# Two small products between gather and output as three products of split operands, on one core

## The chip, the cores and the metric

The kernel runs on one core of a Trainium2 chip. The metric is the device time of one execution in microseconds (us). The engines are TensorE (PE; its weight loads are PEld), VectorE (DVE), ScalarE (ACT), GpSimd (POOL) and SyncE (SP), which issues all DMAs here. Each engine works through its own instructions in the order in which they are written and waits on semaphores for the others.

## The reference, cut to what matters

```python
def _gn(v, G=32, eps=1e-5):                      # group norm over (h, w, 8 channels of a group)
    g = v.reshape(B_, H_, W_, G, C_ // G)
    m = jnp.mean(g, axis=(1, 2, 4), keepdims=True)
    s = jnp.var(g, axis=(1, 2, 4), keepdims=True)
    return ((g - m) / jnp.sqrt(s + eps)).reshape(v.shape)

def conv(x, W_qkv, W_out, b_out):                # x: (16, 64, 64, 256), n = 4096 positions
    qkv = jnp.einsum('bhwc,cd->bhwd', x, W_qkv)
    q, k, v = jnp.split(qkv, 3, axis=-1)         # each to (b, 256, n)
    k = jax.nn.softmax(k, axis=-1)               # over the n positions
    context = jnp.einsum('bdn,ben->bde', k, v)
    out = jnp.einsum('bde,bdn->ben', context, q)
    return jnp.einsum('bhwc,cd->bhwd', out, W_out) + b_out

y = x + conv(_gn(x), W_qkv, W_out, b_out)
```

## The kernel before, in words

The 16 images are done one after the other, as a software pipeline. An image has 4096 positions in 8 chunks of 512 (four tiles of 128), and 256 channels in two halves of 128.

For each image the kernel forms the keys from the raw x with the norm's scale put into the key weights (`wk_hi`, `wk_lo`), takes the exponential of keys less a running maximum (`e_hi`, `e_lo`), and sums exp(keys) times x over positions (the gather). The result, 256 x 256, times `Wq` (`combine_u`) and times `Wv Wout` (`combine_m`, whose weights `wvo` are multiplied out once at the start), plus the identity, is one matrix m. The output is x times m plus a bias. Wherever precision is needed, a factor is split into a high part rounded to fp32r and the rest, and a product is three fp32r products: high by high, low by high, high by low. This holds for the keys (L325 to L360), the gather (L390 to L413) and the output (L447 to L470). The two combines (L419 to L436) are plain fp32 products: `acc` (fp32) by `wq_r`, and `u_sb` (fp32) by `wvo_r`.

TensorE's order in one period (L494 to L533): gather of image b, 8 chunks, with the turning of the second block's maximum in it; keys of chunk 0 of the next image n; `combine_u`; two tiles of keys of chunk 1; `combine_m`; the other two tiles; then output chunks of b and key chunks of n in turn. In the last period there are no keys.

ScalarE splits x and its transpose (`x_hi`, `xt_hi`), copies keys out of PSUM (`keys_out`), does the exponentials, scales `wk`, `wvo` and `wq` (L567 to L584), and adds the output's bias. GpSimd subtracts to get `xt_lo` and `x_lo`; in each period it waits at L315 for `wk_ready` (VectorE's `wk_low`) before the third `xt_low` of the next image, and its order is written out (L305 to L320). VectorE takes the running maximum of keys in `mx`, 512 wide (L731 to L739, two operations a chunk, each waiting for the one before), restarted every four chunks (a block). At the end of a block TensorE turns `mx` with four transposes (L362 to L370), VectorE reduces them to one maximum per channel (L745), and TensorE spreads it (L372). VectorE also shifts the keys (L759), forms `e_lo`, the statistics of the image after next (L693), and the small matrices: `take_second` (L781) leaves `rz` and `acc`, `take_u` (L800) `u_sb`, `take_m` (L808) `m_hi`, `m_full` and `m_lo`.

SP loads the statistics' slots `xs` as VectorE frees them (`bn_done`).

Of the kernel before, what the change touches and what calls it, by code (L numbers as in the profile page):

```python
# [11 lines left out]
P = 128  # L12
# [16 lines left out]
def build(nc: bass.Bass, xt: bass.AP, xn: bass.AP, w: bass.AP, b_out: bass.AP, out: bass.AP):  # L29
# [11 lines left out]
    with ExitStack() as ctx:  # L41
# [33 lines left out]
        wq_t = sb("wq_t", [P, CB, C])  # L75
        wq_r = sb("wq_r", [P, CB, C])
        wvo = sb("wvo", [P, CB, C])
        wvo_r = sb("wvo_r", [P, CB, C])
# [9 lines left out]
        mx = sb("mx", [P, 2 * C])  # L88
        acc = sb("acc", [P, CB, C])
        m_full = acc  # L90
        m_hi = sb("m_hi", [P, CB, C], F32R)
# [3 lines left out]
        m_lo = sb("m_lo", [P, CB, C], F32R)  # L95
# [44 lines left out]
        wvo_r_ready = sem("wvo_r_ready")  # L140
# [22 lines left out]
        wq_r_ready = sem("wq_r_ready")  # L163
# [97 lines left out]
        def _(pool):  # L261
# [64 lines left out]
        def _(pe):  # L326
# [6 lines left out]
            def keys_high(b, parity, j, t0, t1):  # L333
                if t0 == 0:
                    pe.wait_ge(xt_hi_ready, b * NCH + (j + 1))
                    if j == 0:
                        pe.wait_ge(wk_ready, b + 1)
                    if j >= 2:
                        pe.wait_ge(max_done, b * (2 * NCH) + (2 * j - 2))
# [22 lines left out]
            def turn_max(b, blk):  # L362

                to = (ps_g0, ps_k[:, 0])[blk]
                pe.wait_ge(max_done, b * (2 * NCH) + (NCH * blk + NCH))
# [53 lines left out]
            def combine_u(b):  # L419
                pe.wait_ge(wq_r_ready, b * CB + CB)  # L420
                for c in range(CB):
                    for d in range(CB):
                        if c == 0:
                            pe.wait_ge(acc_ready, b * CB + (d + 1))
                        last = nc.tensor.matmul(ps_g0[:, c, 0:C], acc[:, d, c * P:(c + 1) * P], wq_r[:, d, :],  # L425
                                                start=(d == 0), stop=(d == CB - 1))
                    last.then_inc(u_ps, 1)

            def combine_m(b):
                pe.wait_ge(wvo_r_ready, b + 1)  # L430
                pe.wait_ge(u_ready, b + 1)
                for i in range(CB):
                    for c in range(CB):
                        last = nc.tensor.matmul(ps_g0[:, i, 0:C], u_sb[:, c, i * P:(i + 1) * P], wvo_r[:, c, :],  # L434
                                                start=(c == 0), stop=(c == CB - 1))
                    last.then_inc(m_ps, 1)  # L436
# [49 lines left out]
            for j in range(2, NCH):  # L486
                keys(0, 0, j)
                if j == 4:
                    pe.wait_ge(setup_sb, 2)
                    turn_max(0, 0)  # L490
                elif j == 5:
                    spread_max(0, 0)
# [46 lines left out]
        def _(act):  # L539
# [27 lines left out]
            def wvo_scaled(b, parity):  # L567
                act.wait_ge(rstd_ready, b + 1)
                for c in range(CB):
                    last = nc.scalar.activation(wvo_r[:, c, :], wvo[:, c, :], ACT.Copy,  # L570
                                                scale=rstd[:, parity, c:c + 1])
                last.then_inc(wvo_r_ready, 1)

# [6 lines left out]
            def wq_scaled(b):  # L580
                act.wait_ge(rz_ready, b + 1)
                for d in range(CB):
                    nc.scalar.activation(wq_r[:, d, :], wq_t[:, d, :], ACT.Copy,
                                         scale=rz[:, d:d + 1]).then_inc(wq_r_ready, 1)  # L584
# [17 lines left out]
            for j in range(X_SLOTS):  # L602
# [3 lines left out]
                if j == 1:  # L606
                    act.wait_ge(setup_ps, 1)
                    nc.scalar.activation(wvo[:], ps_g0[:, :, 0:C], ACT.Copy).then_inc(setup_sb, 1)
                    act.wait_ge(setup_ps, 2)
                    nc.scalar.activation(wq_sum[:], ps_e[:, 0, 0:C], ACT.Copy).then_inc(setup_sb, 1)  # L610
            act.wait_ge(setup_sb, 2)
# [6 lines left out]
            def period(b, parity, more, more2):  # L618
# [16 lines left out]
                wvo_scaled(b, parity)  # L635
# [6 lines left out]
                wq_scaled(b)  # L642
                if more:
                    keys_out(n, 0, 0)
                    x_high(n, 0)
                    keys_out(n, 0, 1)
                    x_high(n, 1)
# [39 lines left out]
        def _(dve):  # L687
# [43 lines left out]
            def key_max(b, j, h):  # L731
                dve.wait_ge(k_out, b * (2 * NCH) + (2 * j + h + 1))
                if j % HALF == 0 and h == 0:
                    if j or not (isinstance(b, int) and b == 0):
                        dve.wait_ge(t_ps, b * 2 + j // HALF)
                    nc.vector.tensor_copy(mx[:], ps_k[:, j % 2, h, :]).then_inc(max_done, 1)
                    return
                dve.wait_ge(max_done, b * (2 * NCH) + (2 * j + h))
                nc.vector.tensor_tensor(mx[:], ps_k[:, j % 2, h, :], mx[:], ALU.max).then_inc(max_done, 1)  # L739
# [55 lines left out]

            def mean_bias(b, parity):
# [3 lines left out]
            def take_u(b, parity):  # L800
                for c in range(CB):
                    dve.wait_ge(u_ps, b * CB + (c + 1))
                    last = nc.vector.scalar_tensor_tensor(out=u_sb[:, c, :], in0=wq_sum[:],  # L803
                                                          scalar=neg_mean[:, parity, c:c + 1], in1=ps_g0[:, c, 0:C],
                                                          op0=ALU.mult, op1=ALU.add)
                last.then_inc(u_ready, 1)
# [30 lines left out]
            for j in range(HALF):  # L837
                key_maxes(0, j)
                for q in range(2 * j, 2 * j + 2):
                    bn_half(1, q)  # L840
            for q in range(8, 12):
                bn_half(1, q)
# [18 lines left out]
            def period(b, parity, more, more2):  # L861
# [88 lines left out]
```

## Time and profile before

| | us |
|---|---|
| median of 3 runs | 1262.89 (1261.8 to 1263.22) |
| the profiled execution's own time | 1263.93 |
| its span, first to last instruction | 1262.2 |
| granted TensorE clock, mean | 0.996 of full |
| VectorE busy | 879.4 (70%) |
| ScalarE busy | 839.1 (66%) |
| GpSimd busy | 657.4 (52%) |
| DMA | 266.69 MB, mean 211 GB/s |

Times in the trace are from the span's start. In the rows of a timeline, a line is a run of alike instructions: its start, the time from its start to its last end, the engine, the source line, what is written and read, the shapes, and the count. A bracket at the end is the time for which the engine was idle before it, and what released it. Matmuls are pipelined, so a record's duration is longer than its distance to the next.

### The profile page before, as it was taken

The numbers are of one execution on the slowest core, as the hardware profiler recorded it, in microseconds if no ns is written. First come the engines' busy times: TensorE is split into PE (matmuls) and PEld (weight loads), VectorE is DVE, ScalarE is ACT, GpSimd is POOL, SyncE is SP. The second block draws the span as 40 slices with busy tenths as digits, with TensorE's granted clock in tenths as the row PEclk, the third lists the DMA queues.
The fourth block names the chain that finished last, engine by engine and source line by source line (L and its number), as shares of the span: only waits on it lengthen the run. The fifth ranks groups of instructions, "written<-read, shape, count | busy, mean of one in ns | idle before, by whom it ended". The sixth has DMA issues, their size and how long they took to land. (4 is left out here: it accounts for less than half of the span.)

```text
span 1262.2 us, 21236 instructions
## 1 busy us (share of the span) xinstructions
PE 1220.6 (97%) x8396; PEld 1132.2 (90%) x8396; DVE 879.4 (70%) x1264; ACT 839.1 (66%) x1139; POOL 657.4 (52%) x284
## 2 busy tenths in 40 slices
PE   3899999999999999999999999999999999999998
PEld 3798999989999898999989999899999989999886
DVE  5877767877677776767777577676776777577461
ACT  4476857767576776857767576775756768576663
POOL 7274653836546374553736547364563736537320
PEclk9899999999999999999999999999999999999999
DMA  8247657486665867657486564866657576573523
GB/s 332 85 167 267 215 192 245 151 300 217 215 220 170 281 200 258 204 185 260 163 294 209 206 227 157 293 217 236 203 180 265 185 271 219 190 241 118 190 92 134
DMA packets 109107, 266.69 MB, mean 211 GB/s; under 512 B 12240, under 2 KB 12240, under 8 KB 109008
## 3 DMA queue, kind: packets, MB, share of 16 engines
q1 hardware_dynamic: 109008, 265.34, 62.1%
q8 instruction: 66, 1.08, 0.3%
q14 instruction: 33, 0.27, 0.1%
HBM read 198.18 MB, written 67.11 MB: 210 GB/s over the span
## 5 line engine op out<-in xcount | busy, mean ns | idle before, releaser
L283 POOL TENSOR_TENSOR xt_lo<-xt_raw,xt_hi 128x1024 fp32r<-128x1024 f32 x128 | 307.0, 2401 | 496.1 <-ACT xt_hi L543 462.3
L289 POOL TENSOR_TENSOR x_lo<-x_raw,x_hi 128x1024 fp32r<-128x1024 f32 x128 | 324.3, 2548 | 67.5 <-ACT x_hi L548 67.4
L594 ACT ACTIVATE o_stage<-ps_e,bias 128x512 f32<-128x512 f32 x256 | 172.8, 689 | 125.6 <-PE ps_e L463 125.6
L770 DVE TENSOR_TENSOR e_lo<-e_raw,e_hi 128x1024 fp32r<-128x1024 f32 x128 | 251.6, 1966 | 3.1 <-ACT e_raw L561 2.2
L739 DVE TENSOR_TENSOR mx<-ps_k,mx 128x512 f32<-128x512 f32 x224 | 154.7, 691 | 120.6 <-ACT e_raw L552 108.5
L552 ACT ACTIVATE e_raw<-ps_k 128x512 f32<-128x512 f32 x256 | 142.1, 596 | 131.6 <-PE ps_k L328 131.6
L328 PE MATMUL ps_k<-wk_hi,xt_hi 128*128 128x256 f32 x1024 | 214.5, 291 | 3.8 <-DVE wk_lo L725 3.0
L328 PE MATMUL ps_k<-wk_lo,xt_hi 128*128 128x256 f32 x1024 | 207.2, 284 | 0.0
L560 ACT ACTIVATE e_hi<-e_raw 128x1024 fp32r<-128x1024 f32 x128 | 135.0, 1055 | 66.7 <-PE ps_g L409 36.8
L698 DVE BATCH_NORM_STATS2 bn<-xs 128x6 f32<-128x512 f32 x240 | 153.4, 686 | 35.3 <-DMA xs<-in_xt_dram 34.9
L328 PEld LDWEIGHTS ps_k<-wk_hi,xt_hi 128*128 128x128 f32 x1024 | 166.7, 191 | 12.5 <-issue 4.0
L455 PE MATMUL ps_e<-xt_hi,m_hi 128*128 128x512 f32 x512 | 162.3, 398 | 0.6 <-DVE m_hi L811 0.6
L463 PE MATMUL ps_e<-xt_hi,m_lo 128*128 128x512 f32 x512 | 162.1, 398 | 0.0
L455 PE MATMUL ps_e<-xt_lo,m_hi 128*128 128x512 f32 x512 | 160.9, 395 | 0.0
L328 PEld LDWEIGHTS ps_k<-wk_lo,xt_hi 128*128 128x128 f32 x1024 | 159.2, 190 | 0.0
L328 PE MATMUL ps_k<-wk_hi,xt_lo 128*128 128x256 f32 x1024 | 158.5, 283 | 0.0
L548 ACT ACTIVATE x_hi<-x_raw 128x1024 fp32r<-128x1024 f32 x128 | 134.5, 1051 | 17.5 <-DMA x_raw<-in_xn_dram 17.4
L543 ACT ACTIVATE xt_hi<-xt_raw 128x1024 fp32r<-128x1024 f32 x128 | 134.9, 1054 | 4.7 <-DMA xt_raw<-in_xt_dram 4.7
L328 PEld LDWEIGHTS ps_k<-wk_hi,xt_lo 128*128 128x128 f32 x1024 | 137.9, 190 | 0.0
L400 PE MATMUL ps_e<-x_hi,e_hi 128*128 128x258 f32 x512 | 128.8, 290 | 8.7 <-POOL x_lo L289 7.0
L561 ACT ACTIVATE e_raw<-e_raw 128x1024 f32<-128x1024 f32 x128 | 134.1, 1048 | 0.0
L400 PE MATMUL ps_g<-x_hi,e_hi 128*128 128x258 f32 x512 | 126.7, 284 | 3.6 <-issue 3.6
(81 smaller groups left out, 1875.2 us busy)
## 6 DMA issues: line engine op xcount, KB each, us to landing
xt_raw<-in_xt_dram SPq DMA_DIRECT2D x128, 512.0 KB, 4.6
x_raw<-in_xn_dram SPq DMA_DIRECT2D x128, 512.0 KB, 3.4
out_dram<-o_stage SPq DMA_DIRECT2D x256, 256.0 KB, 4.6
xs<-in_xt_dram SPq DMA_DIRECT2D x240, 256.0 KB, 5.0
w_setup<-in_w_dram SPq DMA_DIRECT2D x2, 256.0 KB, 9.7
wk<-in_w_dram SPq DMA_DIRECT2D x1, 256.0 KB, 9.8
wq_t<-in_w_dram SPq DMA_DIRECT2D x1, 256.0 KB, 9.8
b_col<-in_b_out_dram SPq DMA_DIRECT2D x1, 1.0 KB, 9.9
```

The source lines that it names most:

```text
L283: nc.gpsimd.tensor_tensor(xt_lo[:, s], xt_raw[:, s], xt_hi[:, s].bitcast(F32), ALU.subtract).then_inc(xt_lo_ready, 1)
L289: nc.gpsimd.tensor_tensor(x_lo[:, s], x_raw[:, s], x_hi[:, s, :, 0:C].bitcast(F32), ALU.subtract).then_inc(x_lo_ready, 1)
L328: return nc.tensor.matmul(ps_k[:, j % 2, t // 2, (t % 2) * C:(t % 2 + 1) * C], (xt_hi, xt_lo)[xs_][:, slot(j, parity), c, t * P:(t + 1) * ...
L400: nc.tensor.matmul(ps_g[j // HALF][:, d, 0:C + 2], w_, x_hi[:, j % X_SLOTS, t, :], start=(j % HALF == 0 and t == 0), stop=False, skip_grou ...
L455: nc.tensor.matmul(ps_e[:, h, :], m_hi[:, c, h * P:(h + 1) * P], x_[:, s, c, :], start=(n == 0 and c == 0), stop=False, skip_group_check=True)
L463: last = nc.tensor.matmul(ps_e[:, h, :], m_lo[:, c, h * P:(h + 1) * P], xt_hi[:, s, c, :], start=False, stop=(c == CB - 1), skip_group_che ...
L552: nc.scalar.activation(e_raw[:, j, 2 * h:2 * h + 2, :].rearrange("p t c -> p (t c)"), ps_k[:, j % 2, h, :], ACT.Copy).then_inc(k_out, 1)
L560: nc.scalar.activation(e_hi[:, j % E_SLOTS], e_raw[:, j], ACT.Exp).then_inc(e_hi_ready, 1)
L594: nc.scalar.activation(o_stage[:, q % O_SLOTS, :], ps_e[:, h, :], ACT.Identity, bias=bias[:, h:h + 1]).then_inc(o_ready, 1)
L698: nc.vector.bn_stats(bn[:, q % CB, q // CB, :], xs[:, q % S_SLOTS, :]).then_inc(bn_done, 1)
L739: nc.vector.tensor_tensor(mx[:], ps_k[:, j % 2, h, :], mx[:], ALU.max).then_inc(max_done, 1)
L770: nc.vector.tensor_tensor(e_lo[:, j], e_raw[:, j], e_hi[:, j % E_SLOTS].bitcast(F32), ALU.subtract).then_inc(e_lo_ready, 1)
```

## The change

`combine_u` and `combine_m` become three fp32r products each: the left side is split into `acc_hi` and `acc_lo` (`u_hi` and `u_lo`), the right side is split once at the start (`wq_hi`, `wq_lo`, `wvo_hi`, `wvo_lo`). The scales 1/z and rstd, which were put on the right sides in each image by ScalarE, are put on the left sides as they are split: ScalarE writes the high part, VectorE then the low part. GpSimd's wait before the third `xt_low` is for `u_lo_ready` in place of `wk_ready`. The running maximum is 256 wide: four operations a chunk for two, and two transposes a block for four. At the start ScalarE also writes `wq_hi`, and VectorE does two subtractions for `wvo_lo` and `wq_lo`.

```diff
@@ gpsimd, period
-                    pool.wait_ge(wk_ready, n + 1)
+                    pool.wait_ge(u_lo_ready, b * CB + CB)
                     xt_low(n, np_, 2)
@@ tensor
             def turn_max(b, blk):
                 for d in range(CB):
-                    for h in range(2):
-                        last = nc.tensor.transpose(to[:, 0, (2 * d + h) * P:(2 * d + h + 1) * P],
-                                                   mx[:, h * C + d * P:h * C + (d + 1) * P], ident)
+                    last = nc.tensor.transpose(to[:, 0, d * P:(d + 1) * P], mx[:, d * P:(d + 1) * P], ident)
             def combine_u(b):
-                pe.wait_ge(wq_r_ready, b * CB + CB)
                 for c in range(CB):
                     for d in range(CB):
                         if c == 0:
-                            pe.wait_ge(acc_ready, b * CB + (d + 1))
-                        last = nc.tensor.matmul(ps_g0[:, c, 0:C], acc[:, d, c * P:(c + 1) * P], wq_r[:, d, :],
-                                                start=(d == 0), stop=(d == CB - 1))
+                            pe.wait_ge(acc_hi_ready, b * CB + (d + 1))
+                        for w_ in (wq_hi, wq_lo):
+                            nc.tensor.matmul(ps_g0[:, c, 0:C], acc_hi[:, d, c * P:(c + 1) * P], w_[:, d, :],
+                                             start=(d == 0 and w_ is wq_hi), stop=False, skip_group_check=True)
+                for c in range(CB):
+                    for d in range(CB):
+                        if c == 0:
+                            pe.wait_ge(acc_lo_ready, b * CB + (d + 1))
+                        last = nc.tensor.matmul(ps_g0[:, c, 0:C], acc_lo[:, d, c * P:(c + 1) * P], wq_hi[:, d, :],
+                                                start=False, stop=(d == CB - 1), skip_group_check=True)
                     last.then_inc(u_ps, 1)
             (combine_m likewise, with u_hi, u_lo, wvo_hi, wvo_lo)
@@ scalar
-            def wvo_scaled(b, parity): ...
-            def wq_scaled(b): ...
+            def acc_high(b):
+                act.wait_ge(rz_ready, b + 1)
+                for d in range(CB):
+                    act.wait_ge(acc_ready, b * CB + (d + 1))
+                    nc.scalar.activation(acc_hi[:, d, :], acc[:, d, :], ACT.Copy,
+                                         scale=rz[:, d:d + 1]).then_inc(acc_hi_ready, 1)
+            def u_high(b, parity):
+                for c in range(CB):
+                    act.wait_ge(u_ready, b * CB + (c + 1))
+                    nc.scalar.activation(u_hi[:, c, :], u_sb[:, c, :], ACT.Copy,
+                                         scale=rstd[:, parity, c:c + 1]).then_inc(u_hi_ready, 1)
@@ scalar, period
-                wvo_scaled(b, parity)
-                wq_scaled(b)
+                acc_high(b)
                 if more:
                     keys_out(n, 0, 0)
                     x_high(n, 0)
                     keys_out(n, 0, 1)
+                u_high(b, parity)
@@ vector
             def key_max(b, j, h):
                 dve.wait_ge(k_out, b * (2 * NCH) + (2 * j + h + 1))
+                for t in (2 * h, 2 * h + 1):
+                    tile = ps_k[:, j % 2, h, (t % 2) * C:(t % 2 + 1) * C]
+                    if j % HALF == 0 and t == 0:
+                        if j or b:
+                            dve.wait_ge(t_ps, b * 2 + j // HALF)
+                        nc.vector.tensor_copy(mx[:], tile).then_inc(max_done, 1)
+                    else:
+                        dve.wait_ge(max_done, b * (TILES * NCH) + (TILES * j + t))
+                        nc.vector.tensor_tensor(mx[:], tile, mx[:], ALU.max).then_inc(max_done, 1)
+            def acc_low(b):
+                for d in range(CB):
+                    dve.wait_ge(acc_hi_ready, b * CB + (d + 1))
+                    nc.vector.scalar_tensor_tensor(out=acc_lo[:, d, :], in0=acc[:, d, :], scalar=rz[:, d:d + 1],
+                                                   in1=acc_hi[:, d, :].bitcast(F32), op0=ALU.mult,
+                                                   op1=ALU.subtract).then_inc(acc_lo_ready, 1)
+            (u_low likewise, from u_sb, rstd and u_hi)
@@ vector, period
                 take_second(b)
+                acc_low(b)
                 if more:
                     key_max(n, 0, 0)
                 take_u(b, parity)
                 if more:
                     key_max(n, 0, 1)
+                u_low(b, parity)
                 take_m(b, parity)
@@ vector, start, after chunk 1
+                    nc.vector.tensor_tensor(wvo_lo[:], ps_g0[:, :, 0:C], wvo_hi[:].bitcast(F32), ALU.subtract)
+                    nc.vector.tensor_tensor(wq_lo[:], wq_t[:], wq_hi[:].bitcast(F32), ALU.subtract)
```

## Rows read from the trace of the kernel before

**Rows 1.** The page's first part: busy us, share, instructions of each engine.
```profile
PE 1220.6 (97%) x8396; PEld 1132.2 (90%) x8396; DVE 879.4 (70%) x1264; ACT 839.1 (66%) x1139; POOL 657.4 (52%) x284
```
**Rows 2.** TensorE's waits (total, times, longest), and busy times of one image's stretch.
```profile
PE ps_e L400 <- POOL x_lo L289: 7.0, 15, 0.7
...
594.03:670.20 76.17, 75.62 (x525) 70.24 (x524) 55.06 (x80) 52.11 (x71) 41.24 (x17) 1.00 0.66 221
```
**Rows 3.** Timeline of TensorE around the two combines of one image.
```profile
619.64 0.40 PE L328 MATMUL ps_k<-wk_hi,xt_hi 128*128 128x256 f32 x2
...
622.48 1.89 PE L425 MATMUL ps_g<-wq_r,acc 128*128 128x256 f32 x8
624.02 0.59 PE L328 MATMUL ps_k<-wk_hi,xt_hi 128*128 128x256 f32 x2
624.44 0.40 PE L328 MATMUL ps_k<-wk_lo,xt_hi 128*128 128x256 f32 x2
...
629.72 0.95 PE L442 MATMUL ps_g<-neg_mean,acc 128*128 128x1 f32 x8
630.52 0.71 PE L463 MATMUL ps_e<-xt_hi,m_lo 128*128 128x512 f32 x2
```
**Rows 4.** Timeline of TensorE at both turns of the maximum.
```profile
595.95 0.60 PE L368 MATMUL ps_k<-zero_eye,mx 128*128 128x128 f32 x4
596.38 0.28 PE L384 MATMUL ps_k<-mv,grp 128*128 128x2 f32 x2
...
646.63 0.60 PE L368 MATMUL ps_g<-zero_eye,mx 128*128 128x128 f32 x4
```
**Rows 5.** Timeline of VectorE in one image, and in the last.
```profile
609.40 1.90 DVE L770 TENSOR_TENSOR e_lo<-e_raw,e_hi 128x1024 fp32r<-128x1024 f32 x1
...
617.53 0.87 DVE L725 SCALAR_TENSOR_TENSOR wk_lo<-wk,rstd,wk_hi 128x256 fp32r<-128x256 f32 x2
...
620.30 0.85 DVE L793 SCALAR_TENSOR_TENSOR acc<-ps_e,alpha,acc 128x256 f32<-128x256 f32 x2
...
624.41 0.48 DVE L803 SCALAR_TENSOR_TENSOR u_sb<-wq_sum,neg_mean,ps_g 128x256 f32<-128x256 f32 x1 [0.39 <-PE ps_g L425]
...
628.93 1.26 DVE L822 TENSOR_TENSOR m_lo<-acc,m_hi 128x512 fp32r<-128x512 f32 x1
...
644.18 1.49 DVE L739 TENSOR_TENSOR mx<-ps_k,mx 128x512 f32<-128x512 f32 x2 [2.38 <-ACT e_raw L552]
...
667.83 1.49 DVE L739 TENSOR_TENSOR mx<-ps_k,mx 128x512 f32<-128x512 f32 x2 [2.76 <-ACT e_raw L552]
...
1236.22 0.69 DVE L822 TENSOR_TENSOR m_lo<-acc,m_hi 128x512 fp32r<-128x512 f32 x1
```
**Rows 6.** Timeline of ScalarE after a gather.
```profile
620.42 0.91 ACT L583 ACTIVATE wq_r<-wq_t,rz 128x256 f32<-128x256 f32 x2 [4.26 <-DVE rz L790]
621.26 0.60 ACT L552 ACTIVATE e_raw<-ps_k 128x512 f32<-128x512 f32 x1
```
**Rows 7.** Groups by form: count, busy us, mean ns of one, idle before.
```profile
L739 DVE TENSOR_TENSOR mx<-ps_k,mx 128x512 f32<-128x512 f32 x224 | 154.7, 691 | 120.6 <-ACT e_raw L552 108.5 <-DVE mx L739 0.5
...
L776 DVE TENSOR_TENSOR z<-ps_g,alpha 128x2 f32<-128x2 f32 x16 | 2.4, 147 | 1.2 <-PE ps_g L409 1.2
```
**Rows 8.** Timeline of GpSimd in the same image.
```profile
608.01 8.51 POOL L289 TENSOR_TENSOR x_lo<-x_raw,x_hi 128x1024 fp32r<-128x1024 f32 x3
618.48 2.40 POOL L283 TENSOR_TENSOR xt_lo<-xt_raw,xt_hi 128x1024 fp32r<-128x1024 f32 x1 [1.96 <-DVE wk_lo L725]
...
627.45 2.19 POOL L289 TENSOR_TENSOR x_lo<-x_raw,x_hi 128x1024 fp32r<-128x1024 f32 x1 [0.23 <-ACT x_hi L548]
...
640.06 2.41 POOL L283 TENSOR_TENSOR xt_lo<-xt_raw,xt_hi 128x1024 fp32r<-128x1024 f32 x1 [7.24 <-ACT xt_hi L543]
```
**Rows 9.** Timeline of image 0: VectorE's fourth shift, TensorE's first gather.
```profile
56.55 1.22 DVE L764 TENSOR_TENSOR e_raw<-e_raw,ps_g 128x1024 f32<-128x1024 f32 x1
...
57.87 0.55 PE L400 MATMUL ps_g<-x_hi,e_hi 128*128 128x258 f32 x1 [3.58 <-issue]
```

More of the change, by code:

```diff
@@ L74, in build @@
         wk_lo = sb("wk_lo", [P, CB, C], F32R)
[L75 to L78, printed above, removed]
+        with nc.sbuf_tensor("wq_t", [P, CB, C], F32) as wq_t:
+            pass
+        wq_lo = sb("wq_lo", [P, CB, C], F32R)
+        wq_hi = sb("wq_hi", [P, CB, C], F32R)
+        wvo_hi = sb("wvo_hi", [P, CB, C], F32R)
+        wvo_lo = sb("wvo_lo", [P, CB, C], F32R)
         wq_sum = sb("wq_sum", [P, C])
@@ L86, in build @@
         grp = sb("grp", [P, P])
-        mx = sb("mx", [P, 2 * C])
-        acc = sb("acc", [P, CB, C])
+        mx = sb("mx", [P, C])
+        with nc.sbuf_tensor("acc", [P, CB, C], F32) as acc:
+            pass
+        acc_lo = sb("acc_lo", [P, CB, C], F32R)
         m_full = acc
-        m_hi = sb("m_hi", [P, CB, C], F32R)
+        acc_hi = sb("acc_hi", [P, CB, C], F32R)
+        m_hi = acc_hi
         with nc.sbuf_tensor("u_sb", [P, CB, C], F32) as u_sb:
             pass
-        m_lo = sb("m_lo", [P, CB, C], F32R)
+        u_lo = sb("u_lo", [P, CB, C], F32R)
+        u_hi = sb("u_hi", [P, CB, C], F32R)
+        m_lo = u_lo
         bn = sb("bn", [P, CB, NCH, 6])
@@ L162, in build @@
         rz_ready = sem("rz_ready")
-        wq_r_ready = sem("wq_r_ready")
+        acc_hi_ready = sem("acc_hi_ready")
+        acc_lo_ready = sem("acc_lo_ready")
+        u_hi_ready = sem("u_hi_ready")
+        u_lo_ready = sem("u_lo_ready")
+        setup_lo = sem("setup_lo")
         acc_ready = sem("acc_ready")
@@ L431, in combine_m @@
-                pe.wait_ge(u_ready, b + 1)
                 for i in range(CB):
                     for c in range(CB):
-                        last = nc.tensor.matmul(ps_g0[:, i, 0:C], u_sb[:, c, i * P:(i + 1) * P], wvo_r[:, c, :],
-                                                start=(c == 0), stop=(c == CB - 1))
+                        if i == 0:
+                            pe.wait_ge(u_hi_ready, b * CB + (c + 1))
+                        for w_ in (wvo_hi, wvo_lo):
+                            nc.tensor.matmul(ps_g0[:, i, 0:C], u_hi[:, c, i * P:(i + 1) * P], w_[:, c, :],
+                                             start=(c == 0 and w_ is wvo_hi), stop=False, skip_group_check=True)
@@ L436, in combine_m @@
+                for i in range(CB):
+                    for c in range(CB):
+                        if i == 0:
+                            pe.wait_ge(u_lo_ready, b * CB + (c + 1))
+                        last = nc.tensor.matmul(ps_g0[:, i, 0:C], u_lo[:, c, i * P:(i + 1) * P], wvo_hi[:, c, :],
+                                                start=False, stop=(c == CB - 1), skip_group_check=True)
                     last.then_inc(m_ps, 1)
@@ L489, in _ @@
                     pe.wait_ge(setup_sb, 2)
+                    pe.wait_ge(setup_lo, 1)
                     turn_max(0, 0)
@@ L565, in scales @@
                 nc.scalar.activation(alpha[:], dm[:], ACT.Exp).then_inc(alpha_ready, 1)
[L567 to L572, printed above, removed]
             def wk_high(b, parity):
@@ L646, in period @@
                     keys_out(n, 0, 1)
+                u_high(b, parity)
+                if more:
                     x_high(n, 1)
@@ L802, in take_u, with u_low @@
                     dve.wait_ge(u_ps, b * CB + (c + 1))
[L803 to L806, printed above, removed]
+                    nc.vector.scalar_tensor_tensor(out=u_sb[:, c, :], in0=wq_sum[:],
+                                                   scalar=neg_mean[:, parity, c:c + 1], in1=ps_g0[:, c, 0:C],
+                                                   op0=ALU.mult, op1=ALU.add).then_inc(u_ready, 1)
+            def u_low(b, parity):
+                for c in range(CB):
+                    dve.wait_ge(u_hi_ready, b * CB + (c + 1))
+                    nc.vector.scalar_tensor_tensor(out=u_lo[:, c, :], in0=u_sb[:, c, :],
+                                                   scalar=rstd[:, parity, c:c + 1],
+                                                   in1=u_hi[:, c, :].bitcast(F32), op0=ALU.mult,
+                                                   op1=ALU.subtract).then_inc(u_lo_ready, 1)
             def take_m(b, parity):
```

32 lines of the change are left out of this document (15 added, 17 removed).

## The prediction

> **What bounds the kernel now.** I read the busy shares first, then TensorE's waits, then one middle image engine by engine. TensorE is busy 97% of the span [rows 1], and its waits are few: the only one that recurs is 7.0 us in 15 waits for `x_lo`, 0.45 us an image [rows 2]. From one gather's start to the next an image takes 76.17 us, 75.62 of them TensorE work at the full clock [rows 2]. So two questions decide: how much TensorE time the edits take out of an image, and whether the longer chains through ScalarE and VectorE still arrive before TensorE asks for them.
>
> **TensorE work removed.** Key matmuls (fp32r, 256 wide) go at 24 in 622.48 - 619.64 = 2.84 us, 0.118 us each [rows 3]. `combine_u`, four fp32 products, starts at 622.48; the third matmul after it starts at 624.44. Less the two before that (0.24), it costs 1.72 us [rows 3]. Twelve fp32r products of the same width cost 12 x 0.118 = 1.42. Saving 0.30 us each, 0.60 an image. `turn_max` takes 0.43 us for four transposes, up to the next matmul [rows 4]; two less save 0.21, two times an image 0.43. Bounds: the combines save 0.12 if the records' own distance counts (1.54 - 1.42, 624.02 less 622.48), 0.30 with the change-over into fp32r that follows; the transposes 0.18 to 0.21. I take the upper ends, since TensorE's next work starts by them. Together 1.03 us an image.
>
> The Trainium skill, "FP8 and Floating Point Precision", TensorE Precision Notes, says that true FP32 takes four passes through the array. By that four products are 16 passes against 12, and the ratio 16/12 on 1.42 would make the old combine 1.89 and the saving 0.47; the row says 1.72, and the sum goes by the row.
>
> **The chain into `combine_u`.** `rz` comes just before `acc`, which runs 620.30 to 621.15 in two halves [rows 5], and ScalarE's scaled copies take 0.91 for two [rows 6]. New order: `acc_hi` 620.8-621.3 and 621.2-621.7, `acc_lo` on VectorE (two of this kind and width take 0.87 [rows 5]) 621.3-622.2. TensorE asks for `acc_hi` at 622.48 and for `acc_lo` 0.95 later, so 0.6 us and more is to spare: no cost. The cover is the four tiles of keys; without it about 1.9 us would show. ScalarE's `keys_out(n,0,0)` slips from 621.26 [rows 6] to 621.6, and `wvo_scaled` disappears, where ScalarE then idled anyway: nothing on the path.
>
> **The chain into `combine_m`.** The product's second half comes out at 622.48 + 1.42 + 0.2 (as the gather's end reaches VectorE, 619.84 against 619.64) = 624.10. `take_u` is 0.48 a half [rows 5]: 623.9-624.35 and 624.27-624.75. `u_hi` on ScalarE 624.4-624.9, 624.8-625.3; TensorE asks at 625.32 (623.90 + two tiles of keys): in time. Behind `take_u` VectorE still has `key_max(n,0,1)`. No row has a 128x256 maximum; by the 128x512 one (0.691) and the 128x2 operation (0.147) [rows 7] it is 0.42 to 0.43, plus 0.11 from one to the next, which waits for it (two of 0.69 span 1.49 [rows 5]). Two of them: 624.67-625.64. Then `u_lo` 625.56-626.43. TensorE has done its eight high products and one low one at 625.32 + 9 x 0.118 = 626.39 and needs the second half of `u_lo` then, which reaches it at 626.48 to 626.57: a wait of 0.1 to 0.2, with a slow restart of 0.07. I take 0.2 us in each of 15 images. Bounds: 0 if the narrow maximum takes half of 0.691 (0.35), 0.7 if it takes all of it.
>
> **GpSimd, moved behind `u_lo`.** It started `xt_low(n,2)` at 618.48 [rows 8], now at 626.5. Everything on its queue behind that moves too: four `x_low` of 2.2 and `xt_low(n,3)`. 2.4 + 0.6 + 4 x 2.2 puts it free at 638.3; `xt_low(n,3)` waited 7.24 us for ScalarE until 640.06 [rows 8]. SP issues nothing in this step that waits for GpSimd. No cost from lateness, but the order matters for `m_lo`. Two-input SBUF operations of VectorE and GpSimd's subtractions never share a stretch here: `e_lo` took 1.90 when it started at 609.40 [rows 5], within GpSimd's three `x_lo` of 8.51 us from 608.01 [rows 8]: 0.8 of waiting for the one in flight, then 1.1 of work, while the next one stood. `m_lo` likewise took 1.26 at 628.93 against 0.69 in the last image, where GpSimd is idle [rows 5]; the `x_lo` in flight ended at 629.64 [rows 8].
>
> Now call T the end of `u_lo`. GpSimd's `xt_lo` runs T+0.08 to T+2.47. TensorE resumes at T+0.1, `m_hi`'s halves end at T+0.98 and T+1.38, the two `m_full` at T+2.17, `m_lo` is issued at T+2.27: 0.2 us before GpSimd's instruction ends. It goes next and is done at T+3.0. TensorE asks for it at T+0.53 (combine over) + 1.42 (keys) + 0.94 + 0.80 (high products and bias sum, 628.78 to 630.52 in this image, [rows 3] has the bias sum's start and the end) = T+3.7. No cost, and 0.6 us earlier than today.
>
> The Trainium skill, "SBUF — State Buffer", Who interferes with whom, states this as a rule: a VectorE instruction with two SBUF inputs contends with a GpSimd one that reads SBUF, and issue order decides who blocks. The durations above agree. By it `acc_lo` and `u_lo` are safe, as GpSimd is idle there, and `m_lo` hangs on which GpSimd instruction it meets.
>
> **The narrower maximum on VectorE.** Four operations for two: 3 x 0.54 + 0.43 = 2.05 against 1.49, 0.56 us a chunk, 4.5 an image. VectorE idles 2.76 us before the last chunk's maximum at 667.83 [rows 5]; the chunks whose delay reaches it (4, 5, 6) add 1.7, and the wait shrinks to about 1. Before the first block's turn: chunk 3 starts at 644.18 and would end at 646.23; TensorE turns at 646.63 [rows 4]: 0.3 to spare after 0.14 of signalling. The reduction of a turned block is 0.27 shorter, off the path. No cost in steady state. Upper bound, at 0.69 each: 3.1 a chunk, turn 0.8 late.
>
> **Start.** In image 0 VectorE is the bound: the fourth `shift` at 56.55 lasts 1.22, and TensorE starts the first gather at 57.87 after 3.58 us idle [rows 9]. From the first block's reduction, some 12 us earlier, VectorE is never idle, and three chunks of maxima (+1.7), less 0.3 for the reduction, lie in it. Ahead of it the two set-up subtractions (1.3) and wider maxima delay the statistics that free `xs` slots, by some 0.9. Gather starts 2.3 us later; bounds 1.2 and 4.
>
> **Sum.** 15 full images at -1.03 + 0.2 = -0.83 give -12.5; the last one has no keys for cover, but its added splits overlap its high products: -0.4 with its one `turn_max`. Start +2.3. Together -10.6 us, on the profiled execution's own 1263.93 us (span 1262.2 and 1.7 around it): 1253.3. That execution lies 1.04 above the median of the runs, 1262.89, and the same step from the median gives 1252.3; I say 1253.
>
> **Rivals.**
> (a) `m_lo` misses its turn. If it is issued over 0.2 us later against GpSimd, or GpSimd sooner, it meets `x_low(n,0)`, waits 2.2 us more, ends at T+5.2, and TensorE, at T+3.7, waits 1.65 us with the signalling: 15 x 1.65 = 25, time 1278. For it: the small distance and GpSimd's queue that is now full behind `xt_lo`. Against: both ends hang on the same T, and their durations repeat to 0.02 us. From 0.2 us on it decides. Slower.
> (b) VectorE late. A narrow maximum that costs 0.48 (as the two-scalar operations of this width) and splits that come some tenths later put 0.5 us on the `u_lo` wait and 0.2 on the turn, and 1.5 on the start: 15 x 0.5 + 1.5 = 9 less gain, 1262. For it: `u_lo` is already the last to come. Against: the cheaper two-input rows.
> (c) No wait at all, and the start hidden: 1253.3 - 3 - 1 = 1249. For it, the 0.1 us by which I find the wait; against, that VectorE's order is fixed.
> (d) The change doesn't save: twelve products with their weight loads go at 0.19 like the old records (1.54 for eight): 2.3 against 1.72, +0.6 x 30 = 18, time 1271 with the transposes' saving inside. Against: keys, with a new weight load for each product, hold 0.118.
>
> **Numbers.** Forecast 0.60, (a) 0.13, (b) 0.12, (c) 0.12, (d) 0.03. The forecast's own range is 1250 to 1257; with (c) and (b) 1248 to 1263, leaving out (a) and (d). A difference under 0.2% (2.5 us) can't be told from none. Faster holds forecast, (c) and a third of (b): 0.76; same, most of the rest of (b): 0.07; slower 0.17.
>
> **What would show it.** Distance from `combine_u`'s first product to the next key 1.42 and 12 records in it; a wait of TensorE for `u_lo` of 0.1 to 0.2, some 15 times; the maximum at 0.43; `m_lo` under 1 us and ended before `x_low(n,0)` starts (2 us or more is rival (a)); the first gather at about 60.2; the `x_lo` wait unchanged at 0.45. The prediction is wrong if an image isn't 0.6 to 1.1 us shorter than 76.2.

## The result and the profile after

The changed kernel takes 1252.12 us (median of 4 runs, 1248.38 to 1255.10) against 1262.47 (median of 4, 1261.8 to 1263.22). The ratio is 0.9917, 95% interval 0.9901 to 0.9934. The profiled execution took 1255.10, span 1253.3.

The page's first part answers to [rows 1], the wait and the stretch of one image to [rows 2]. The stretch runs again from one gather's start to the next.

```profile
PE 1210.3 (97%) x8460; PEld 1127.4 (90%) x8460; DVE 932.3 (74%) x1586; ACT 838.0 (67%) x1140; POOL 661.3 (53%) x284
...
PE ps_e L409 <- POOL x_lo L300: 7.2, 15, 0.5
...
587.92:663.12 75.20, 74.62 (x530) 69.61 (x529) 58.48 (x100) 51.98 (x71) 41.58 (x17) 1.00 0.67 224
```

TensorE is still the bound, the `x_lo` wait is still there, and an image is 0.97 us shorter. VectorE has 3.4 us more work in it and none of it shows.

The timeline of TensorE around the turn and the two combines, answering to [rows 3, 4]. In the trace of the changed kernel `acc_hi` also stands for `m_hi` and `u_lo` for `m_lo`, which share their memory.

```profile
589.83 0.38 PE L378 MATMUL ps_k<-zero_eye,mx 128*128 128x128 f32 x2
590.05 0.28 PE L393 MATMUL ps_k<-mv,grp 128*128 128x2 f32 x2
...
616.12 0.28 PE L436 MATMUL ps_g<-wq_hi,acc_hi 128*128 128x256 f32 x1
...
617.08 0.63 PE L442 MATMUL ps_g<-wq_hi,acc_lo 128*128 128x256 f32 x4
617.55 0.39 PE L339 MATMUL ps_k<-wk_hi,xt_hi 128*128 128x256 f32 x2
...
618.97 0.28 PE L452 MATMUL ps_g<-wvo_hi,u_hi 128*128 128x256 f32 x1
...
619.93 0.73 PE L458 MATMUL ps_g<-wvo_hi,u_lo 128*128 128x256 f32 x4
620.50 0.39 PE L339 MATMUL ps_k<-wk_hi,xt_hi 128*128 128x256 f32 x2
```

The turn takes 0.22 us for 0.43. `combine_u` takes 617.55 - 616.12 = 1.43, and the key after it starts at once. `combine_m` takes 1.53: its last four records, 0.73 long in place of 0.63, hold a wait of 0.10 for `u_lo`.

VectorE and GpSimd in the same stretch, answering to [rows 5, 8]:

```profile
618.31 0.88 DVE L767 TENSOR_TENSOR mx<-ps_k,mx 128x256 f32<-128x256 f32 x2
619.10 0.87 DVE L845 SCALAR_TENSOR_TENSOR u_lo<-u_sb,rstd,u_hi 128x256 fp32r<-128x256 f32 x2
...
622.22 0.79 DVE L864 TENSOR_TENSOR u_lo<-acc,acc_hi 128x512 fp32r<-128x512 f32 x1
...
623.91 1.87 DVE L767 TENSOR_TENSOR mx<-ps_k,mx 128x256 f32<-128x256 f32 x4
```
```profile
620.05 2.41 POOL L294 TENSOR_TENSOR xt_lo<-xt_raw,xt_hi 128x1024 fp32r<-128x1024 f32 x1 [9.87 <-DVE u_lo L845]
622.42 9.13 POOL L300 TENSOR_TENSOR x_lo<-x_raw,x_hi 128x1024 fp32r<-128x1024 f32 x4
```

`m_lo` (the `u_lo` of L864) is issued at 622.22, 0.24 us before GpSimd's `xt_lo` ends at 622.46. It waits a tenth of a us and takes 0.79, where it took 1.26 before. The four `x_lo` take 9.13 together, so the first stood behind `m_lo`.

The whole difference of the two profiled executions (1263.93 - 1255.10 = 8.83) splits by the starts of the gathers:

| stretch | before | after | difference |
|---|---|---|---|
| to the first gather | 57.87 | 58.38 | +0.5 |
| 15 images, first gather to last | 1145.59 | 1131.30 | -14.3 |
| last gather to the last matmul's start | 54.86 | 59.78 | +4.9 |

The images gained more than forecast (12.5), and the last image lost what nobody had counted. The first row can't be read from one pair: over the ten traces here whose kernels have the changed start the first gather comes anywhere from 56.64 to 59.63, and the kernel before, with the same start, gave 56.47 in another trace (that of `before with fill` below).

For the last image the granted clock shows why. The first fence is the changed kernel from within its last gather to the end, the second the kernel before at the same distance from its end (TensorE busy, its granted clock, DMA).

```profile
1203.50:1217.00 13.50, 11.30 (x89) 1.00 0.09 33
1217.00:1230.50 13.50, 12.24 (x44) 0.50 0.05 19
1230.50:1249.50 19.00, 19.00 (x83) 0.99 0.47 180
```
```profile
1217.30:1230.80 13.50, 11.33 (x89) 1.00 0.09 34
1230.80:1244.30 13.50, 12.26 (x57) 1.00 0.20 77
```

For 13.5 us TensorE ran at 1.2 in place of 2.4 GHz. It has three waits in the last image alone, where no keys stand between the products:

```profile
PE ps_g L436 <- ACT acc_hi L602: 1.6, 1, 1.6
...
PE ps_g L452 <- ACT u_hi L608: 0.7, 1, 0.7
PE ps_e L479 <- DVE acc_hi L853: 0.6, 1, 0.6
```

Only the first of them lies ahead of the fall. `combine_u` starts at 1216.25, after the 1.62 us wait, and the clock falls within its first products; the two shorter waits come when it is already at half:

```profile
1216.25 0.39 PE L436 MATMUL ps_g<-wq_hi,acc_hi 128*128 128x256 f32 x1 [1.62 <-ACT acc_hi L602]
```
```profile
1216.50:1217.00 0.50, 0.50 (x5) 1.00 0.00 0
1217.00:1217.50 0.50, 0.50 (x5) 0.59 0.00 0
1217.50:1218.00 0.50, 0.50 (x5) 0.50 0.00 0
```

The kernel before waited as long at the same places and kept 2.4 GHz:

```profile
1230.19 1.99 PE L425 MATMUL ps_g<-wq_r,acc 128*128 128x256 f32 x8 [1.58 <-ACT wq_r L583]
1232.85 1.97 PE L434 MATMUL ps_g<-wvo_r,u_sb 128*128 128x256 f32 x8 [0.67 <-DVE u_sb L803]
1235.39 0.73 PE L455 MATMUL ps_e<-xt_hi,m_hi 128*128 128x512 f32 x2 [0.58 <-DVE m_hi L811]
```

### The profile page after: what moved, and what is told of

Same layout as the page of the kernel before. It is cut to its first block, busy times and chain, and to the rows that moved or that the text cites. A ratio compares the mean times of both kernels' runs of the same rounds, so it can differ in the third digit from the quotient of the medians.

```text
span 1253.3 us, 21671 instructions
## 1 busy us (share of the span) xinstructions
PE 1210.3 (97%) x8460; PEld 1127.4 (90%) x8460; DVE 932.3 (74%) x1586; ACT 838.0 (67%) x1140; POOL 661.3 (53%) x284
## 4 chain that ended last, share of the span: by engine, by line
PE 79%; POOL 9%; DMA 4%; ACT 3%; DVE 3%; issue 1%; SPq 0%; ACTq 0%; DVEq 0%; POOLq 0%
PE ps_k L339 28%; PE ps_e L479 19%; PE ps_e L487 10%; POOL x_lo L300 6%; PE ps_e L409 4%; PE ps_e L418 4%; PE ps_e L411 3%; DMA x_raw<-in_xn_dram 3%; POOL rstd L305 2%; POOL xt_lo L294 2%; PE ps_g L418 2%; PE ps_g L409 2%; PE ps_g L411 2%; PE ps_g L452 1%; PE ps_g L436 1%
## 5 line engine op out<-in xcount | busy, mean ns | idle before, releaser
L300 POOL TENSOR_TENSOR x_lo<-x_raw,x_hi 128x1024 fp32r<-128x1024 f32 x128 | 328.2, 2587 | 20.6 <-ACT x_hi L573 20.1
L767 DVE TENSOR_TENSOR mx<-ps_k,mx 128x256 f32<-128x256 f32 x480 | 203.4, 424 | 99.6 <-ACT e_raw L577 78.7
L798 DVE TENSOR_TENSOR e_lo<-e_raw,e_hi 128x1024 fp32r<-128x1024 f32 x128 | 247.4, 1934 | 4.9 <-ACT e_raw L586 4.5
L339 PE MATMUL ps_k<-wk_hi,xt_hi 128*128 128x256 f32 x1024 | 208.6, 285 | 4.2 <-DVE wk_lo L751 3.0
L479 PE MATMUL ps_e<-xt_hi,acc_hi 128*128 128x512 f32 x512 | 163.7, 401 | 1.0 <-DVE acc_hi L853 0.6
L487 PE MATMUL ps_e<-xt_hi,u_lo 128*128 128x512 f32 x512 | 163.1, 400 | 0.0
L479 PE MATMUL ps_e<-xt_lo,acc_hi 128*128 128x512 f32 x512 | 161.6, 397 | 0.0
```

The lines of the kernel that those rows point to most:

```text
L300: nc.gpsimd.tensor_tensor(x_lo[:, s], x_raw[:, s], x_hi[:, s, :, 0:C].bitcast(F32), ALU.subtract).then_inc(x_lo_ready, 1)
L339: return nc.tensor.matmul(ps_k[:, j % 2, t // 2, (t % 2) * C:(t % 2 + 1) * C], (xt_hi, xt_lo)[xs_][:, slot(j, parity), c, t * P:(t + 1) * ...
L479: nc.tensor.matmul(ps_e[:, h, :], m_hi[:, c, h * P:(h + 1) * P], x_[:, s, c, :], start=(n == 0 and c == 0), stop=False, skip_group_check=True)
L487: last = nc.tensor.matmul(ps_e[:, h, :], m_lo[:, c, h * P:(h + 1) * P], xt_hi[:, s, c, :], start=False, stop=(c == CB - 1), skip_group_che ...
L767: nc.vector.tensor_tensor(mx[:], tile, mx[:], ALU.max).then_inc(max_done, 1)
L798: nc.vector.tensor_tensor(e_lo[:, j], e_raw[:, j], e_hi[:, j % E_SLOTS].bitcast(F32), ALU.subtract).then_inc(e_lo_ready, 1)
```

## The experiments

Each run's own median, with the ratio to the kernel before on the same chip. The third number, an image, is the usual distance of two gather starts in the profile; it is 76.18 before and 75.22 after. The last, the end, is the distance from the last gather's start to the last matmul's start, 54.86 before and 59.78 after. Where two values stand for an image, the first is that of the images at full clock and the second that of those with a stretch at half clock. What each run changes is told below the table; a "fill" is matmuls that nobody reads, put into a wait.

| | us | ratio, 95% interval | image | end |
|---|---|---|---|---|
| changed kernel | 1252.12 | 0.9917, 0.9901 to 0.9934 | 75.22 | 59.78 |
| narrow maximum alone | 1257.73 | 0.9962, 0.9950 to 0.9974 | 75.73 | 54.66 |
| split combines alone | 1258.27 | 0.9951, 0.9935 to 0.9968 | 75.57 | 60.13 |
| fill, three waits | 1250.07 | 0.9900, 0.9887 to 0.9913 | 75.23 | 54.81 |
| before with fill | 1262.55 | 0.9999, 0.9990 to 1.0008 | 76.18 | 54.01 |
| fill, first wait | 1249.19 | 0.9888, 0.9874 to 0.9902 | 75.23 | 54.85 |
| maximum after `u_lo` | 1282.79 | 1.0162, 1.0141 to 1.0184 | 76.3 / 77.75 | 59.83 |
| the same, `x_lo` held | 1249.72 | 0.9902, 0.9877 to 0.9927 | 75.11 | 54.80 |
| `m_lo` later | 1297.00 | 1.0272, 1.0253 to 1.0292 | 76.8 / 78.3 | 59.80 |
| GpSimd's wait put back | 1286.35 | 1.0184, 1.0167 to 1.0201 | 76.5 / 78.0 | 59.82 |
| `rstd` later | 1250.97 | 0.9911, 0.9891 to 0.9931 | 75.22 | 54.81 |
| fill, held, `rstd` later | 1249.74 | 0.9894, 0.9879 to 0.9908 | 75.11 | 54.81 |
| fill first, held | 1248.71 | 0.9890, 0.9873 to 0.9906 | 75.11 | 54.82 |

**The two halves.** The kernel before with the new `key_max`, `turn_max` and `block_max` alone:

```diff
-        mx = sb("mx", [P, 2 * C])
+        mx = sb("mx", [P, C])
+                for t in (2 * h, 2 * h + 1): ...          # as in the change
```


> The kernel before with the 256-wide maximum alone. My account: two transposes less at each of 31 turns, 0.21 us each, -6.6; the start +0.5 as in the changed kernel's trace; together -6, and an image of 75.75 us for 76.17. No half-clock stretch in the last image, since the fp32 combines stay. Rival: the narrow maximum is what loses clock or start time (the start +2.3 as I forecast), then -4 or less.

It came to 1257.73, -4.9 against 1262.65. An image is 75.73, -0.45, as two turns of 0.21 say, and the end is unchanged. The first gather came at 58.86, 1.0 later than before where I had said 0.5; that is within what the same start does from run to run (56.64 to 59.63), so it doesn't say why the whole is 4.9 and not 6.

The changed kernel with the wide maximum back, so the split combines alone:

```diff
-        mx = sb("mx", [P, C])
+        mx = sb("mx", [P, 2 * C])
-                        for w_ in (wvo_hi, wvo_lo):
+                        for w_ in (wvo_hi, wq_lo):
```


> The changed kernel with the 512-wide maximum, so the split combines alone (for room the low part of wvo is not kept, combine_m reads the low part of wq in its place: same work, other numbers). My account: 0.30 us at each of 30 combines, -9, and the u_lo wait gone or under 0.1; an image of 75.57. The last image may lose up to 6.7 us at half clock: then -2 to -9 in all. If the half clock belongs to the split combines, it shows here and not with the maximum alone.

An image is 75.57, -0.61: two combines of 0.30. The runs fall into two groups by the mean granted clock: 1252.86 and 1253.07 at 0.997, and four from 1257.73 to 1259.09 at 0.992. The profiled run is one of the four, and in it the half clock lies in the last image (its end is 60.13); that the other three lost it there too is inferred from their mean. So -9.7 where the end keeps its clock, as I had it, and -4.4 in the median, where it doesn't. The half clock comes with the split combines. The two halves add to -1.06 an image, both together give -0.96: the 0.10 left is the `u_lo` wait, which only the two together have.

**The end.** The changed kernel with matmuls that nobody reads in the last image's waits:

```diff
+            def fill(parity, k):
+                for i in range(k):
+                    nc.tensor.matmul(ps_k[:, 1, 0, 0:C], xt_hi[:, slot(4, parity), i % CB, 0:P], wk_hi[:, i % CB, :],
+                                     start=True, stop=True, skip_group_check=True)
                 if more:
                     keys_tiles(n, np_, 0, 0, 4)
+                else:
+                    fill(parity, 12)
                 combine_u(b)
+                (likewise 5 before combine_m, 4 before the output)
```


> The changed kernel, and in the last image alone 12, 5 and 4 extra matmuls whose result nobody reads, put into TensorE's three waits before combine_u, combine_m and the output. If the waits cost the last image its clock (1217 to 1230 at half clock in the changed kernel's trace, 6.7 us), the granted clock stays full there and the time falls to 1246, with a smaller spread over the runs. Rival: the runs' spread (1248 to 1255) is from elsewhere, and the extra work changes nothing or adds up to 1 us.

The end fell back to 54.81 at full clock, -5.0. The median is 1250.07, higher than I expected, since I had taken the whole 6.7 us of half clock off the median, in which only some runs had it, and the end itself had lost 5.0, not 6.7. The intervals of this kernel (0.9887 to 0.9913) and of the changed one (0.9901 to 0.9934) overlap, so the gain is shown by the end's length and by the clocks counted below, not by the medians. The three waits shrank to 0.2, 0.3 and 0.3 us.

> The kernel before with the same extra matmuls in its last image. Its trace held full clock there, so no change within 1 us. If it also becomes faster, its own runs lose clock too and the fill's worth is not a matter of the split combines.

In the kernel before the same fill shows no gain in time: ratio 0.9999 over 11 runs. Its end is 0.85 shorter in the profile than without, which the interval (0.1% either way, 1.2 us) can't exclude.

> The changed kernel with the twelve extra matmuls in the first of the last image's three waits alone. If the first, 1.6 us long, is what costs the clock, the last image holds full clock as with all three filled (1250). If the shorter two matter as much, the half clock comes back in most runs (1255).

Filling the first wait alone is enough, as the place of the fall within the first products says too. This is its stretch over the first products (TensorE busy, granted clock), and the two waits that stay:

```profile
1213.00:1226.50 13.50, 11.68 (x63) 1.00 0.15 58
```
```profile
PE ps_g L452 <- ACT u_hi L619: 0.9, 1, 0.9
...
PE ps_e L479 <- DVE acc_hi L864: 0.7, 1, 0.7
```

Over all kernels with the short combine chain and without fill (changed, split alone, `x_lo` held, `rstd` later), 9 of 20 runs had a mean clock of 0.992 or less, and they are the longest ones of each: 1255.10 and 1253.51 against 1250.72 and 1248.38 in the changed kernel. Of 18 runs with fill none had, and none took over 1252.1. The mean clock is only a sign of it, since every trace also has some half clock before the second image; where the half clock lay is known for the profiled runs, and there it is at the end for the two at 0.992 or less and not for the other two. The kernel before isn't free of it altogether: one of its 46 runs had 0.993 and took 1267.17, 4.2 us over the median of its group, and where its clock fell no trace shows.

**The rival that was priced at 1278.** First the edit that looks like a gain: take the maximum out of `u_lo`'s way.

```diff
                 take_u(b, parity)
+                u_low(b, parity)
                 if more:
                     key_max(n, 0, 1)
-                u_low(b, parity)
```


> The changed kernel with the maximum of the second key tiles moved from before u_lo to after it, on VectorE. u_lo then comes 0.4 us earlier or more, TensorE no longer waits for it. By the exclusive order of VectorE's and GpSimd's two-input subtractions GpSimd starts earlier too, m_lo is issued just after x_low of the next image began, waits 2.2 us for it, and TensorE waits some 1.5 us in each of 15 images: +22, 1274, an m_lo of 2.5 us or more. Rival, if the engines share rather than exclude: -1 to -2 us, 1251.

1282.79, slower by 20.7 us against the kernel before, 31 against the changed one, and 9 more than the 1274 expected. VectorE, GpSimd and TensorE of one image:

```profile
634.00 0.88 DVE L845 SCALAR_TENSOR_TENSOR u_lo<-u_sb,rstd,u_hi 128x256 fp32r<-128x256 f32 x2 [0.19 <-ACT u_hi L608]
...
637.55 2.52 DVE L864 TENSOR_TENSOR u_lo<-acc,acc_hi 128x512 fp32r<-128x512 f32 x1
```
```profile
634.96 2.41 POOL L294 TENSOR_TENSOR xt_lo<-xt_raw,xt_hi 128x1024 fp32r<-128x1024 f32 x1 [9.38 <-DVE u_lo L845]
637.33 4.81 POOL L300 TENSOR_TENSOR x_lo<-x_raw,x_hi 128x1024 fp32r<-128x1024 f32 x2
```
```profile
640.13 0.72 PE L487 MATMUL ps_e<-xt_hi,u_lo 128*128 128x512 f32 x2 [1.01 <-DVE u_lo L864]
...
641.76 1.06 PE L487 MATMUL ps_e<-xt_hi,u_lo 128*128 128x512 f32 x2
642.62 0.63 PE L339 MATMUL ps_k<-wk_hi,xt_hi 128*128 128x256 f32 x2
643.05 0.63 PE L339 MATMUL ps_k<-wk_lo,xt_hi 128*128 128x256 f32 x2
```

`u_lo` ends at 634.88 and releases GpSimd, whose `x_lo` starts at 637.33. `m_lo` is issued at 637.55, 0.2 us too late, and takes 2.52. TensorE waits 1.01. And then, from 641.8, its matmuls stand 0.43 apart by twos in place of 0.24, half clock. That comes in 9 of the last 14 images, which take 77.75; the other 5 take 76.3. So the wait costs 1.1 us an image, by the mechanism expected (I had 1.5), and the clock after it another 1.45 in most, which I hadn't counted.

The same edit, and GpSimd held:

```diff
                     xt_low(n, np_, 2)
+                    pool.wait_ge(m_lo_ready, b + 1)
                     for j in range(X_SLOTS):
```


> The same move, and GpSimd waits for m_lo before x_low of the next image. If the block is m_lo's meeting with x_low, the cost of the last one vanishes and what is left is the u_lo wait saved: -1 to -1.5 us against the changed kernel, m_lo at 0.69 to 0.9. If the move costs for another reason (the maximum being late), the cost stays.

```profile
619.17 0.88 DVE L768 TENSOR_TENSOR mx<-ps_k,mx 128x256 f32<-128x256 f32 x2
...
621.92 0.69 DVE L865 TENSOR_TENSOR u_lo<-acc,acc_hi 128x512 fp32r<-128x512 f32 x1
```
```profile
619.33 2.41 POOL L294 TENSOR_TENSOR xt_lo<-xt_raw,xt_hi 128x1024 fp32r<-128x1024 f32 x1 [9.38 <-DVE u_lo L846]
622.69 4.37 POOL L300 TENSOR_TENSOR x_lo<-x_raw,x_hi 128x1024 fp32r<-128x1024 f32 x2 [0.95 <-DVE u_lo L865]
```

`m_lo` takes 0.69 and an image 75.11, 0.11 less than in the changed kernel. The two kernels differ in one wait, and by 33 us in the medians. Of the 37.1 us between their profiled executions 31.9 lie in the 15 images: one meeting of two instructions, and what the clock makes of it. The other 5.0 are the half clock at the end, which this profile doesn't have. The late maximum itself shows no cost.

From the other side, with `m_lo` pushed back behind other work of VectorE:

```diff
             def take_m(b, parity): ...
                 last.then_inc(m_full_ready, 1)
+                if b < B - 1:
+                    key_max(b + 1, 1, 0)
                 dve.wait_ge(m_hi_ready, b + 1)
```


> The changed kernel with two 256-wide maxima of the next image's chunk 1 moved ahead of m_lo (0.9 us). m_lo, issued 0.24 us before GpSimd's xt_lo ends now, is issued 0.6 us after it and meets x_low(n,0): it ends about 2.2 us later than now, and TensorE waits 1.5 us an image: +22. Rival, without the block: m_lo ends 0.9 later, at the point where TensorE asks for it: +0 to +2.

1297.00, where I had expected 22 more than the changed kernel, 1274. `m_lo` takes 2.34, and TensorE's wait for it is 1.4 us in each of 15 images.

```profile
640.80 2.34 DVE L866 TENSOR_TENSOR u_lo<-acc,acc_hi 128x512 fp32r<-128x512 f32 x1
```
```profile
640.40 6.95 POOL L300 TENSOR_TENSOR x_lo<-x_raw,x_hi 128x1024 fp32r<-128x1024 f32 x3
```

An image at full clock takes 1.54 more than in the changed kernel, 23 us in 15 images, as expected. But 12 of the last 14 images run in part at half clock, at 1.5 us each, and these 18 us I hadn't counted. In this run and in `maximum after u_lo` `m_lo` ends 2.74 us after the start of the `x_lo` that it met, though it was issued 0.40 after that start here and 0.22 there.

And GpSimd's wait as it was before the change:

```diff
-                    pool.wait_ge(u_lo_ready, b * CB + CB)
+                    pool.wait_ge(wk_ready, n + 1)
```


> The changed kernel with GpSimd's wait put back to wk_low (as before the change): xt_low(n,2) early, then x_low(n,0..3) each as x_hi comes. By the intervals of the trace u_lo finds GpSimd idle (619.04 to 619.9) but m_lo, issued at 622.22, meets x_low(n,2) begun at 622.14, and ends at 624.9 where TensorE asks for it at 623.7: +1.3 us an image, +19, 1271. Rival: the moved wait has no effect on time, 1252.

1286.35, for 1271 expected. Again the price of the wait is right, 1.27 us an image at full clock and 19 in 15, and what is missing is the half clock, in 10 of the last 14 images. The groups of waits of these two kernels, in this order:

```profile
PE ps_e L487 <- DVE u_lo L866: 21.1, 15, 1.4
```
```profile
PE ps_e L487 <- DVE u_lo L864: 17.1, 15, 1.2
```

In this last kernel `m_lo` takes 2.67:

```profile
635.44 2.68 DVE L864 TENSOR_TENSOR u_lo<-acc,acc_hi 128x512 fp32r<-128x512 f32 x1
```

Without the moved wait the change would have been slower than before by 1.8%.

**The wait for `x_lo`.** One attempt at the recurring wait of [rows 2]:

```diff
                     x_low(b, j)
-                    if j == HALF and more:
+                    if j == HALF + 1 and more:
                         rstd_of(n, np_)
```


> The changed kernel with GpSimd's rstd of the next image moved from before to after x_low of chunk 5, in the gather. It took 1.67 us there, ahead of the x_lo for which TensorE waits 0.48 us in each of 15 images (and restarts slowly at chunks 6 and 7, 0.2 each). The gather's bound is GpSimd's queue: -0.5 to -0.9 an image, -7 to -13 in all. Rival: the block between e_lo and x_lo moves along and another x_lo becomes late: 0 to -3; or wk_hi comes late on ScalarE: slower.

An image stays at 75.22: the rival came true, another `x_lo` became late. The rows show where the 1.7 us went. GpSimd, free earlier, waits 0.68 for ScalarE's `x_hi` before chunk 5's `x_lo`, and `rstd` then stands ahead of chunk 6's. TensorE's wait of 0.48 at chunk 5 is gone and one of 0.71 at chunk 6 stands in its place; in all it now waits 8.8 us for `x_lo` and 2.1 for ScalarE's `e_hi`, for 7.2 before the edit.

```profile
599.16 2.48 POOL L300 TENSOR_TENSOR x_lo<-x_raw,x_hi 128x1024 fp32r<-128x1024 f32 x1 [0.68 <-ACT x_hi L573]
601.59 1.69 POOL L305 TENSOR_TENSOR rstd<-var_eps,neg_half 128x2 f32<-128x2 f32 x1
```
```profile
PE ps_e L409 <- POOL x_lo L300: 8.8, 13, 0.7
...
PE ps_e L409 <- ACT e_hi L585: 2.1, 3, 0.7
```

**Together.** The three edits in one kernel:

> The changed kernel with the three edits together: extra matmuls in the last image's waits, the maximum after u_lo with GpSimd's x_low held for m_lo, and rstd after x_low of chunk 5. If they add: the full-clock end (1250.2), -0.11 an image (-1.6), and what the rstd edit gives (-7 to -13): 1236 to 1242. If the x_lo wait doesn't move: 1249.

1249.74, and an image of 75.11: the `rstd` edit brings nothing here either. Without it, and with the first wait's fill alone:

> The changed kernel with the twelve extra matmuls ahead of the last image's first product, the maximum after u_lo, and GpSimd's x_low held for m_lo. If the two add: images of 75.11 us for 75.22 (-1.6) and the last image at full clock: 1247.5 to 1249, with all runs at a granted clock of 0.995 or more. If one cancels the other: 1249 to 1250.

1248.71, images of 75.11, end 54.82, four runs at 0.994 to 0.999. The two edits add in the trace. In the medians this version, 0.9890, can't be told from the first-wait fill alone, 0.9888; both are faster than the kernel before by 1.1%. Against the changed kernel's 0.9917 their intervals overlap.

## Why the prediction came out right

Forecast 1253, measured 1252.12. By its steps:

- **TensorE work removed**: right, 1.06 us an image for 1.03. 0.30 a combine and 0.21 a turn were the upper ends of my bounds, and the halves run alone gave 0.61 and 0.45 an image. What comes after a stretch in another format belongs to its price: the fp32 products' cost was 1.72, not the 1.54 between first records.
- **Chain into `combine_u`**: right, no wait.
- **Chain into `combine_m`**: right in place, half in size, 0.10 for 0.2. The narrow maximum took 0.424, as interpolated, but the two of one `key_max` call start with 0.04 us between them, not 0.11: two rows of 0.42 span 0.88. Only from one call to the next is it 0.10. This mis-sized wait is most of why an image gained 0.96 and not 0.83.
- **GpSimd moved, `m_lo`**: right, to the tenth: 0.24 us of margin for 0.2, 0.79 us. Rival (a) was a real mechanism next door: two edits of the order by less than 1 us each, and the wait put back, all set it off. Its wait was priced nearly right where `u_lo` kept its place, 1.54 us an image in `m_lo` later for 1.65; in the other two it is 1.07 and 1.27. What it left out is the half clock behind the wait, 1.5 us in 9 to 12 of the last 14 images, so the three came to 1283 to 1297 and not to 1278.
- **Start**: wrong in size. +2.3 was forecast with a lower bound of 1.2; the profiled pair shows +0.5, but the first gather moves by up to 3 us between traces with the same start, so the whole term can't be read from it. One part repeats in every trace: from the first block's reduction to the fourth `shift` it is 11.67 us in the three traces with the wide maximum and 12.54 to 12.56 in the eleven with the narrow one. That is 0.88 for the 1.4 forecast (1.7 less 0.3). The term that failed is the chunks of maxima: 1.86 each and not 2.05, so three cost 1.1 and not 1.7. The 0.9 for the statistics' slots is not shown: in the pair the last of them is done earlier, at 44.60, and the fourth `shift` starts at 57.07 against 56.55 [rows 9], while the reduction moves from 42.78 to 45.77 between traces of the same start.

```profile
43.28 1.32 DVE L724 BATCH_NORM_STATS2 bn<-xs 128x6 f32<-128x512 f32 x2 [0.94 <-DMA xs<-in_xt_dram]
...
54.16 1.86 DVE L767 TENSOR_TENSOR mx<-ps_k,mx 128x256 f32<-128x256 f32 x4
...
57.07 1.21 DVE L792 TENSOR_TENSOR e_raw<-e_raw,ps_g 128x1024 f32<-128x1024 f32 x1
```

- **Last image**: wrong. -0.4 was forecast, +4.9 measured. I laid the products out at full clock through waits of 1.6, 0.7 and 0.6 us, because the kernel before had kept it there. The first of them was followed by half clock.
- **Sum**: -10.6 forecast. The parts of the profiled pair are +0.5, -14.3 and +4.9, so it is right in part because errors cancel: 3.6 us too much time in the forecast for the start and the images (1.8 each), 5.3 too little for the end. That 1253 lies within 1 us of the median is luck: the median of four runs stands between two that kept the clock, 1250.72 and 1248.38, and two that lost it, 1253.51 and 1255.10.
- **Rivals' sums**: (b) leaves its 0.2 on the turn out of its 9 us. (d) is too low: twelve products at 0.19 are 2.3, 0.86 over the forecast's 1.42, so 30 combines add 26 to 1253 and give 1279, not 1271. Neither came: the products stand at 0.12, the narrow maximum at 0.42. (c) takes 1 us for a hidden start that had been put at 2.3.

The Trainium skill, "SBUF — State Buffer", Who interferes with whom, has the rule that decided the four runs from `maximum after u_lo` on: the pair of ports that VectorE shares with GpSimd is an exclusive lock, and the order of issue decides who blocks. The traces agree: one instruction took 0.79 and 0.69 us where it was issued before GpSimd's next `x_lo` of 2.2 us began, and 2.52, 2.34 and 2.67 where it was issued after.

What stays open is why the split combines lose the clock at the end in about half of the runs, where the fp32 ones nearly always keep it after waits of the same length. The fill shows that TensorE's first wait is needed for it; it doesn't show what differs in the products.

## What to carry to other kernels

Where two engines exclude each other by instruction, a chain made shorter can be a loss. Write down for each such instruction which one of the other engine is in flight when it is issued, with the margin, and pin the order with a wait if the margin is tenths of a us. Price a wait of TensorE not by its length alone: after 1 us and more the clock may be half for several us, in some images or some runs and not in others. Check the last iteration by itself, since what covers a chain in all others is missing there. And a sum that comes out right isn't evidence for its terms: split the result at the same boundaries as the forecast, and look at more than one trace before reading a term from a difference of 0.5 us.

## What the runs showed of the hardware

- A wait of 1.0 us of TensorE in a stream otherwise dense was followed by half clock in 9 of 14 images, one of 1.1 in 10 of 14, one of 1.4 in 12 of 14: three kernels, the same place. After the `x_lo` wait of 0.48 us the changed kernel's granted clock is 1.00 in all of its last 14 images.
- Of four maxima of 128x256 on VectorE that each wait for the one before, the two on one half of the keys' tile start 0.04 us apart from end to start, and from one half to the other it is 0.10. At 128x512, one to a half, it was 0.11.
- A VectorE subtraction of 0.69 us that was issued 0.22 or 0.40 us after a GpSimd subtraction of 2.2 us began ended 2.74 us after that beginning both times.
- Four fp32 transposes of 128x128 cost TensorE 0.43 us, two 0.22.
- Work without use in an idle gap can pay: 12 matmuls in 1.4 us of a 1.6 us gap kept the clock, which is worth 5 us here in the runs that lose it. No run with fill shows the loss (0 of 18), 9 of 20 without do.
